# A Mamba stage in which TensorE fills two pairs of PSUM banks in a row instead of one

## The reference, cut to what matters

```
xb, z = split(x @ in_w.T)
xb    = silu(causal_conv(xb, 4 taps) + conv_b)
delta = softplus(dt_part(xb) @ dtw.T + dtb);  Bm, Cm = parts of xb @ xp_w.T
dA    = exp(delta * -exp(a_log))              # per channel and state
mi    = delta * Bm * xb
v_t   = 0.6 * v_(t-1) + mi_t                  # first recurrence, a fixed factor
h_t   = dA_t * h_(t-1) + v_t                  # second recurrence
y_t   = sum over the 16 states of h_t * C_t
out   = ((y + Dp * xb) * silu(z)) @ out_w.T
```

## Time and profile before

| | us |
|---|---|
| median of three runs | 1530.66 |
| the profiled execution, in all | 1527.98 |
| its span | 1526.5 |
| TensorE (PE) busy | 1373.7 (90%) |
| VectorE (DVE) busy | 1056.8 (69%) |
| ScalarE (ACT) busy | 898.0 (59%) |
| GpSimd (POOL) busy | 926.8 (61%) |
| additions, PE L614, two name groups of hst alone | 238.2 in 1596 matmuls |
| scans, DVE L783 | 463.4 in 399 and 133.3 in 113 |
| multiplications, POOL L990 | 510.9 in 399 and 145.7 in 113 |

### The profile page before, as it was taken

The page is one execution under the profiler, slowest core; times in us unless marked ns, Lnnn a source line. Parts: engine busy times, 40 slices in busy tenths (PEclk is TensorE's granted clock), DMA queues, the critical chain, the costliest instruction groups (busy, mean ns, idle before and its releaser), DMA issues.

```text
span 1526.5 us, 46972 instructions
## 1 busy us (share of the span) xinstructions
PE 1373.7 (90%) x20570; PEld 972.8 (64%) x20570; DVE 1056.8 (69%) x1339; ACT 898.0 (59%) x1309; POOL 926.8 (61%) x809
## 2 busy tenths in 40 slices
PE   4679999999999999999999987789898887999997
PEld 2357677767767767777777765444434343599996
DVE  3299998798888887887986895676676761522224
ACT  3757767767766776786677663145555565434440
POOL 1269898989989989989989968500303000045441
PEclk8789999999999999999999998889999999999999
DMA  4111222221322212221221354540606001512225
GB/s 139 48 56 59 86 86 85 86 84 60 113 85 85 82 62 85 85 87 61 82 86 68 145 135 127 94 104 1 112 14 111 0 1 61 223 53 69 67 67 182
DMA packets 41498, 127.28 MB, mean 83 GB/s; under 512 B 8784, under 2 KB 21584, under 8 KB 32848
## 3 DMA queue, kind: packets, MB, share of 16 engines
q1 hardware_dynamic: 34736, 108.28, 21.8%
q0 software_dynamic: 6048, 14.95, 3.7%
q10 hardware_dynamic: 512, 1.05, 0.4%
HBM read 97.90 MB, written 9.57 MB: 70 GB/s over the span
## 4 chain that ended last, share of the span: by engine, by line
PE 47%; DVE 27%; ACT 10%; issue 8%; POOL 3%; DMA 3%; SPq 1%; DVEq 0%; ACTq 0%
DVE hst L783 12%; PE psum L635 6%; PE psum L614 4%; PE psum L1301 4%; PE psum L1713 4%; PE psum L1725 4%; DVE overlay L683 3%; DVE w_early L783 3%; PE psum L1283 2%; PE psum L576 2%; ACT dA L919 2%; PE psum L516 2%; POOL hst L990 2%; PE psum L1655 2%; PE psum L1267 2%
## 5 line engine op out<-in xcount | busy, mean ns | idle before, releaser
L990 POOL TENSOR_TENSOR hst<-hst,cb 128x512 f32<-128x512 f32 x399 | 510.9, 1304 | 99.0 <-DVE hst L783 84.2
L783 DVE TENSOR_TENSOR_SCAN hst<-dA,psum 128x512 f32<-128x512 f32 x399 | 463.4, 1201 | 119.5 <-PE psum L635 119.3
L614 PE MATMUL psum<-ident,hst 128*128 128x128 f32 x1596 | 238.2, 284 | 15.3 <-POOL hst L990 12.6
L919 ACT ACTIVATE dA<-delta,alog 128x512 f32<-128x512 f32 x256 | 177.7, 718 | 84.7 <-DVE hst L783 64.7
L614 PEld LDWEIGHTS psum<-ident,hst 128*128 128x128 f32 x1596 | 176.1, 143 | 62.4 <-issue 21.1
L919 ACT ACTIVATE dA<-xres,alog 128x512 f32<-128x512 f32 x256 | 176.3, 718 | 63.2 <-DVE hst L783 49.6
L1422 DVE TENSOR_REDUCE nmax<-psum 128x2 f32<-128x1024 f32 x128 | 154.7, 1220 | 57.4 <-PE psum L1267 57.1
L1351 ACT ACTIVATE pT<-psum 128x1024 f32<-128x1024 f32 x128 | 127.9, 1024 | 103.6 <-PE psum L1287 80.3
L635 PE MATMUL psum<-filt,c_early 64*64 64x86 f32 (+1 forms) x6144 | 147.3, 242 | 19.8 <-DVE hst L783 11.0
L635 PEld LDWEIGHTS psum<-filt,c_early 64*64 64x64 f32 x6144 | 126.7, 136 | 57.3 <-issue 38.6
L635 PE MATMUL psum<-filt,uT 64*64 64x86 f32 (+1 forms) x6144 | 145.1, 239 | 14.8 <-DVE hst L783 7.6
(11 more groups left out here) (231 smaller groups left out, 2108.9 us busy)
## 6 DMA issues: line engine op xcount, KB each, us to landing
cb<-c_rows SPq DMA_DIRECT2D x64, 1024.0 KB, 4.8
qk_first<-w_early SPq DMA_DIRECT2D x64, 64.0 KB, 2.4
qk<-part SPq DMA_DIRECT2D x64, 64.0 KB, 2.8
w_up<-up_dram SPq DMA_DIRECT2D x8, 512.0 KB, 7.5
w_down<-down_dram SPq DMA_DIRECT2D x8, 512.0 KB, 13.2
w_up<-y_choice SPq DMA_DIRECT2D x8, 512.0 KB, 6.7
qk<-part POOLq DMA_DIRECT2D x48, 64.0 KB, 5.1
qk_first<-part SPq DMA_DIRECT2D x40, 64.0 KB, 2.4
```

The costliest lines, as they stand in the source:

```text
L614: m = pe.matmul(psum[:, Y0 + et % EP, t * P:(t + 1) * P], hst(i)[:, t * P:(t + 1) * P], ident[:], start=n == 0 and t == 0, stop=n == NSTAT ...
L783: dve.tensor_tensor_scan(hst(i), a, v, 0.0, ALU.mult, ALU.add).then_inc(scan_done, 1)
L919: act.activation(dA[:, a % NDA, :], delta[k % 2][:, et, :], ACT.Exp, scale=alog[:, k // B, et, n:n + 1]).then_inc(decay_done, 1)
L990: pool.tensor_tensor(h, h, cb[:, q % 2, state_of(i)[1] % GN, :], ALU.mult).then_inc(g_done, 1)
```

## The change

TensorE now works in runs of VRUN = 4 states. Order for a run that begins at i: fill of (i, i + 1); fill of (i + 2, i + 3); chunk-end stages due in the run; then for o = i to i + 3 the addition of o - 7 and the other side steps of o. The ring is laid out by this order. The chunk-end stages move from 50, 54, 58 to 52, 56, 60, and ScalarE's copies of them from s + n to s + 1 + n. The semaphore `y_full`, raised once for a finished sum, becomes `added`, raised by every addition; VectorE's scan of state i now waits for the addition of state i - 9, whose buffer it overwrites (before, the order of fills and additions implied that). The readers of y and two DMAs wait for the matching counts of `added`.

```diff
-            NDA, AHEAD, LAG, NRING, Y0 = 5, 4, 7, 6, 6
+            NDA, AHEAD, LAG, NRING, Y0, VRUN = 5, 4, 7, 6, 6, 4
...
-                for part, s in (("e1", 50), ("e2", 54), ("e3", 58)):
+                for part, s in (("e1", 52), ("e2", 56), ("e3", 60)):
                     for n in range(len(STAGES[part])):
                         put(s, "pe", part, n)
-                        put(s + n, "act", part, n)
+                        put(s + 1 + n, "act", part, n)
...
-            for i in range(0, NI * TILES, 2):
-                rows += [(("v", i), "scan"), (("v", i + 1), "scan")]
+            for i in range(0, NI * TILES, VRUN):
+                rows += [(("v", o), "scan") for o in range(i, i + VRUN)]
                 for tiled in (True, False):
-                    rows += [(x, TAKER[x[1]]) for x in pair_steps(i) if (x[1] in TILED) == tiled]
+                    rows += [(x, TAKER[x[1]]) for x in run_steps(i) if (x[1] in TILED) == tiled]
...
-                if n == NSTATE - 1:
-                    m.then_inc(y_full, 1)
+                m.then_inc(added, 1)
+
+            def pe_pair(i):
+                k, n, et = state_of(i)
+                f = NPAIRS * k + n // 2
+                if i % TILES == 0:
+                    pe.wait_ge(bank_act, emptied_by("act", k, "e3", 0))
+                if i % (2 * EP) == 0:
+                    pe.wait_ge(filt_done, f + 1)
+                halves_at = [...]
+                ...                                  # the matmuls of L635, as before
...
-                for i in range(NI * TILES):
...
-                    if i % 2 == 0:
-                        ...                          # the fill of the pair
-                        for x in pair_steps(i):
-                            if x[1] in TILED:
-                                pe_side(*x)
-                    if i >= LAG:
-                        pe_add_state(i - LAG)
-                    for x in steps["pe"].get((k, i % TILES), []):
-                        if x[1] not in TILED:
-                            pe_side(*x)
+                for i in range(0, NI * TILES, VRUN):
+                    for o in range(i, i + VRUN, 2):
+                        pe_pair(o)
+                    for x in run_steps(i):
+                        if x[1] in TILED:
+                            pe_side(*x)
+                    for o in range(i, i + VRUN):
+                        if o >= LAG:
+                            pe_add_state(o - LAG)
+                        for x in steps["pe"].get((o // TILES, o % TILES), []):
+                            if x[1] not in TILED:
+                                pe_side(*x)
...
                     dve.wait_ge(decay_done, i + 1)
+                    if i >= NH:
+                        dve.wait_ge(added, i - NH + 1)
...
-                    act.wait_ge(y_full, ET * k + j + 1)
+                    act.wait_ge(added, TILES * k + (j // EP + 1) * EP * NSTATE - 2 * (EP - 1 - j % EP))
...
-                sp.wait_ge(y_full, ET * NI)
+                sp.wait_ge(added, TILES * NI)
```

More of the change, by code:

```diff
@@ L264, in build @@
             zeroed, u_done, gated, gated_dve, filt_done = (sem(n) for n in ("zeroed", "u_done", "gated", "gated_dve", "filt_done"))
-            bank_full, v_full, y_full = sem("bank_full"), sem("v_full"), sem("y_full")
+            bank_full, v_full, added = sem("bank_full"), sem("v_full"), sem("added")
             bank_dve, bank_act = sem("bank_dve"), sem("bank_act")
@@ L468, in at_steps, with run_steps @@
                 return [x for s in range(TILES) for x in steps[engine].get((at, s), [])]
-            def pair_steps(i):
-                return [x for o in (i, i + 1) for x in steps["pe"].get((o // TILES, o % TILES), [])]
+            def run_steps(i):
+                return [x for o in range(i, i + VRUN) for x in steps["pe"].get((o // TILES, o % TILES), [])]
             TAKER = {"xn": "dve", "p": "dve", "z": "act", "xp": "act", "dbcT": "dve", "d": "act", "u": "act", "e1": "act", "e2": "act", "e3": "act", "bt": "dve", "bo": "dve", "ak": "dve", "aq": "dve", "ax": "act"}
             rows = [(x, TAKER[x[1]]) for x in at_steps("pe", "first")]
-            for i in range(0, NI * TILES, 2):
-                rows += [(("v", i), "scan"), (("v", i + 1), "scan")]
+            for i in range(0, NI * TILES, VRUN):
+                rows += [(("v", o), "scan") for o in range(i, i + VRUN)]
                 for tiled in (True, False):
-                    rows += [(x, TAKER[x[1]]) for x in pair_steps(i) if (x[1] in TILED) == tiled]
+                    rows += [(x, TAKER[x[1]]) for x in run_steps(i) if (x[1] in TILED) == tiled]
             rows += [(x, TAKER[x[1]]) for x in at_steps("pe", "last")]
@@ L615, in pe_add_state @@
                                   start=n == 0 and t == 0, stop=n == NSTATE - 1, is_transpose=True, skip_group_check=True)
-                if n == NSTATE - 1:
-                    m.then_inc(y_full, 1)
+                m.then_inc(added, 1)
[6 more added lines that the diff above has]
+                    pe.wait_ge(filt_done, f + 1)
+                halves_at = [pe_open("v", i + half).rearrange("p (t n) -> p n t", n=2) for half in range(2)]
+                for c, (t0, width) in enumerate(CHUNKS):
+                    for e0 in range(0, P, MT):
+                        for half in range(2):
+                            r0 = half * KT
+                            m = pe.matmul(halves_at[half][e0:e0 + MT, :, t0:t0 + width], uT[k % 2][r0:r0 + KT, c, et * P + e0:et * P + e0 + MT],
+                                          filt[r0:r0 + KT, f % NFILT, c, :, 0:width], start=True, stop=True, tile_position=(r0, e0))
+                            if c == NCH - 1:
+                                m.then_inc(v_full, 1)
             def pe_mamba():
```

## The result

The changed kernel takes 1581.97 us (median of four runs, 1572.66 to 1584.11) against 1531.29 for the kernel before in the same job: ratio 1.0309, interval 1.0279 to 1.0339. By the medians it is slower by 50.7 us (3.3%), by the recorded ratio by about 47: some eleven times the forecast loss of 4.5, and outside the range. The direction was right, the size wrong. The profiled execution took 1583.05 with a span of 1581.6, so its span is 55.1 above that of before.

A forecast was written before the change was run, and what follows sets the result against it. TensorE was taken to bound each chunk's first 76.1 us, VectorE the other 32.8. Terms +2.2, +13.2, -11.4 and -0.6 gave +3.4, with rounded waits +4.5: 1532.5 by the profiled run, 1535 as median, range 1518 to 1547.

The forecast's parts named there:

- Part 1, the price of a switch: TensorE's changes between small and full tiles: 0.30 us saved per round trip, 12 in a chunk's first regime, 3.6 us.
- Part 2, first regime: Silu to about 404 us, TensorE busiest: 3.6 less 2.1 of bank waits, plus 0.4 at next chunk: 1.9 us gained.
- The sum: First chunk +2.2, six second regimes +13.2, six first regimes -11.4, last chunk -0.6: +3.4, with rounded waits +4.5 us.
- Part 2, second regime: From 404 us to next silu, VectorE busy: third convolution late behind fill 14, 2.2 us lost in each of six chunks.
- Part 3, first chunk: VectorE's scan 54 waits behind e1, 2.3 us late; fill 60 adds about 1.3; net loss 2.2 us.
- Part 4: Chunk-end stages two states later: 0 to 0.2 us at the next chunk's first fill, up to 1 if ScalarE is held.
- Part 3's "increments and waits cost 0": Increments on added ride on matmuls, 0; VectorE's new wait costs nothing in the first regime, bounds 0 and 1.7 us.
- more waits: Rival: VectorE's waits push nearly full GpSimd until its backlog reaches the additions, 1.5 us more a chunk, 1546; chance 0.10.
- the two large terms: Six second regimes losing 2.2 us each, +13.2, against six first regimes gaining 1.9 each, -11.4.

The follow-up runs named there:

- mixed_c0_small_c: Changed kernel with pairs in the whole first chunk (stages back) and in states 0 to 15 of the others, later C-row loads cut to one partition: 1526.43 us.
- warm_small_c: Changed kernel with C-row loads after the first two cut to one partition and two extra matmul calls before fill 14 in six chunks: 1551.95 us.
- after: The changed kernel itself, with runs of four states and the real C-row loads: 1581.97 us.
- stages_small_c: Changed kernel with pairs again, chunk-end stages still two states later, C-row loads after the first two cut to one partition: 1542.08 us.
- sem_only: Changed kernel with pairs and chunk-end stages back at 50, 54, 58, leaving only the counting on added and VectorE's wait: 1533.22 us.
- after_warm: Changed kernel with two unneeded matmul calls put into TensorE's wait ahead of fill 14 in six chunks: 1564.07 us.
- p2_early: Changed kernel with the third p matmul group at state 11 instead of 12, ahead of fill 14: 1565.35 us.

## Why the prediction was wrong, point by point

**Part 1, the price of a switch: right for the part that a row shows.** Two fills in a row and the addition behind them, TensorE in order of time:
```profile
361.89 2.01 PE L630 MATMUL psum<-filt,c_early 64*64 64x86 f32 x96
363.83 1.09 PE L614 MATMUL psum<-ident,hst 128*128 128x128 f32 x8
```
1.94 from start to start, 1.95 forecast: the 0.15 between a fill and an addition is saved. What all 0.30 of a round trip are worth is the next point.

**Part 2, first regime: right sign, a third to half of the size.** In a chunk of 107.9 of `mixed_c0_small_c`, one of the three best, with nothing else disturbed, TensorE and ScalarE in order of time:
```profile
411.93 1.12 PE L637 MATMUL psum<-filt,uT 64*64 64x86 f32 x48
```
```profile
442.63 1.92 ACT L838 ACTIVATE overlay<-overlay 128x2048 f32<-128x2048 f32 x1 [0.18 <-DVE overlay L693]
```
Its silu before is at 334.75. From the silu to the next chunk's first fill it is 411.93 - 334.75 = 77.18, against 405.84 - 327.93 = 77.91 before: -0.7, where I had 1.5. From there to the silu it is 30.70 against 31.00: -0.3, where I had -0.4. The mean of its five later periods is 108.3, so over all of them the gain is 0.6 a chunk, not 1.9. (The sum counts six first regimes and the rivals seven, a difference of 1.9 us in all.) TensorE's waits grew by 1.15 only, less than my 2.1 (0.88, 1.38, 0.61, 0.63 and 0.25 against 2.60 in all before), so its own work shrank by 1.9 and not by 12 x 0.30 = 3.6. In four of the runs the second fill waits for its bank (0.88, 0.61, 0.63 and 0.25 us ahead of fills 22, 38, 42 and 58; 1.1 and 0.6 were forecast for the first two). A change of tiles saved in front of such a wait can gain nothing; that this is the reason is argued, and which others did not pay is open.

**Part 2, second regime: the right place, sized at the wrong clock.** This is the first step that failed. The term 2.2 a chunk is what `warm_small_c` shows (2.20). In after it is 3.50 to 4.83, since the wait that I had written off as free (TensorE idle for a bank while VectorE is the bound) puts TensorE at its 1.2 GHz level, and the group behind it is on the path: 3.43 - 1.88 = 1.6 for L516 and some tenths for the fill and the addition. In the order of before TensorE stands 0.75 there and does not slow. The forecast said that TensorE stands at fill 14 with two additions undone, but never asked what this does to the clock. Alone, with small loads, filling the wait gives 7.7 us.

**Part 3, first chunk: mechanism right, 13.7 in place of 2.2 (11.5 against the slowest first chunk of the old order).** Fill 54's wait for scan 51 and scan 54's wait behind `e1` are there. Behind the 4.42 of wait come 1.64 for 1.12, 5.32 for 2.78 and about 0.4 more for the first addition: 3.5 of clock on the 2.3 of order, which is the forecast's figure, is 5.8, and the trace has 5.99. The rest (a second wait before L516 of 2.44 at 191.41, and the slow clock at the chunk's head behind a wait of 3.31) I had at 1.3. Going back to pairs there gives 10.0 to 12.6.

**Part 4: wrong where it stands alone, small in the sum.** I asked only whether the next chunk's first fill comes late. In pairs, moving the stages costs 1.7 a chunk (`stages_small_c`); moving a user of the ring deals all later banks anew. In runs of four the first regime shows no such loss (77.18).

**Part 3's "increments and waits cost 0": right**, by `sem_only`.

**The missing term.** This is the second step that failed, and the largest single piece: no step of the sum, and no rival, had TensorE held up by the large loads, 18 to 20 us. The sum treated "the same matmuls, nearer together" as a gain by definition. In the kernel before nothing warned of it as idle time: no row there ends with "issue" between 110 and 900 us, and taking its loads away gives only 4.5 us.

The Trainium skill, Runtime: NRT & Kernel Launch, section Instruction fetch mechanics, says that an engine's instructions come in blocks of 256 by the sequencer's own DMA queue and that this is mostly hidden. For dense tiled matmuls the runs here disagree: 17.6 us of idle time marked "issue", 18 to 20 us gained when the large loads go. Two of the gaps in after, at 284.41 and 294.93, are 253 matmuls and 254 weight loads apart, which is two blocks of 256 less five. By that page's block an estimate is that a u group (64 matmuls and 64 weight loads in 1.09 us, 287.54 to 288.63) uses one up in 2.2 us, less than half the time that a C load takes to land (4.7 to 4.9 in the rows between 250 and 300 us). The same section gives TensorE room for 2048 instructions, eight such blocks; by this rate that is an estimate of 17 us, so the rate alone does not explain the gaps. How far ahead the instructions had been fetched no run here shows.

Of the rivals, "more waits" (1546) came nearest and for the wrong reason: in the changed kernel no group of TensorE's idle times between 110 and 900 us is ended by GpSimd. That the direction came out right is in part luck, since the two large terms nearly cancelled and most of the loss came from what the sum left out.

Open: by which path a large load holds back TensorE's instructions; what fixes whether the clock falls behind a given wait (1.39 us was enough once, and 1.61 was not); what makes some chunks of the small-load runs 0.7 to 1.9 us longer than their neighbours, beyond the two stretches shown; and how the first chunk's loss divides between order and clock outside the stretch shown.

## What to carry to other kernels

An idle gap on TensorE is not free because another engine is the bound: if what follows the gap is on the path, price it at the 1.2 GHz level too, and ask of every reordering whether it makes one gap of 3.5 us out of several short ones. Packing small matmuls closer raises the demand for instructions, and here it brought gaps of up to 2.8 us where large loads fell; look where large loads land against the densest groups before counting the gain. And when buffers are dealt in order of use, moving one user two places is a change of every wait behind it.

## What the runs showed of the hardware

- TensorE's clock stayed at 1.00 behind waits of 1.61 us at fill 14 in `after_warm` and `warm_small_c`, and was near 0.5 for parts of the stretch behind waits of 2.86 (`p2_early`) and 3.52 (after). Four matmuls of 1.98 us in all, in the gap, were the whole difference. Without the large loads they were worth 7.7 us; with them 18, of which the fall of the "issue" idle from 17.6 to 5.4 is a part. A wait's length alone does not decide: in `warm_small_c` the clock stayed at 1.00 behind most waits of 1.39 and was at 0.53 behind the one at 700.00.
- A 1 MB load (4.7 to 4.9 us from issue to landing) was followed by a stop of TensorE of 0.9 to 2.8 us that no semaphore ends, up to some 2 us after its last packet (landed about 282, matmuls again at 284.41). Half-size loads still gave 1.2 to 1.7. Without the loads no such stop of 0.8 us or more is left.
- A stop of this kind costs more than its length where the clock falls behind it: 2.52 us at 643.01 in after, then `e1` at 4.41 instead of 2.78.
